# Probability products of an attention kernel issued for two tiles at a time instead of one

## The chip, the cores and the metric

The kernel runs on one core of a Trainium2 chip. The metric is the device time of one launch in microseconds (us). Three runs gave 1793.2, 1794.21 and 1794.51 us, median 1794.21. Below, PE is TensorE, DVE is VectorE, ACT is ScalarE, POOL is GpSimd, and SP issues the DMAs.

## The reference, cut to what matters

The input is 4 sequences (b) of 1024 tokens and width 512. A post-norm layer is computed: causal attention with 32 heads of 16 dimensions, then a linear layer on values rounded to 4 bits in blocks.

```python
q, k, v = x @ Wq.T, x @ Wk.T, x @ Wv.T         # 32 heads of 16; q, k get rotary positions
scores = einsum('bhid,bhjd->bhij', q, k) * scale
scores = scores + bias        # learnable, for 0 <= i - j < 256, and 0 outside that band
scores = where(i >= j, scores, -inf)
m = maximum(max(scores, -1), softmax_offset)
p = exp(scores - m)
denom = sum(p, -1) + exp(softmax_offset - m)
out = einsum('bhij,bhjd->bhid', p, v) / denom
x = layernorm(x + out @ Wo.T)
x = layernorm(x + quantised_linear(x))
```

The change is in how `p @ v` is ordered among the other products. Nothing else is touched.

## The kernel before, in words

There are three stages. Stage 1 (up to about 415 us) makes q, k and v and stores them. Stage 2 (about 415 to 1507 us) is the attention. Stage 3 is the two layer norms and the linear layer. The change is in stage 2 alone.

Stage 2 is 32 **steps**: 8 groups (g) of 4 heads, by 4 sequences (b), n = 4g + b. A step is cut into 12 **tiles** T. A tile is one block of 128 keys by up to 512 queries, transposed (keys on partitions), for all 4 heads. `TILES` gives the order: tiles 0 to 3 are the first 512 queries (512, 384, 256 and 128 queries wide, since the causal corner is left out), tiles 4 to 11 are the second 512 queries (512 wide for tiles 4 to 8, then 384, 256, 128). Ten of the twelve tiles touch the band in which the bias is not zero (`BANDED`, all but tiles 4 and 5).

A tile is worked off as two **units** u = 2T and 2T + 1, of two heads each, so a step has 24 units. The work of one step on each engine:

- PE, `scores` (lines 663 to 689): two score products (line 679), one per head, into the bank pair `ps_s[u % 2]`. There are two bank pairs, so scores of unit u wait until the exponential of unit u - 2 is done (line 669). For an even unit of a banded tile PE also adds the bias by two products with an identity (line 685). For an odd unit of a banded tile ACT has written the bias into the bank pair first (`seed`), and PE waits for that (line 676).
- ACT, `exp_unit` (lines 871 to 877): one exponential over both heads of the unit, from `ps_s` to `probs`, which holds three tiles. Behind an odd unit comes `seed` (lines 879 to 892) for the next tile: a fill with zeros outside the band (line 889) where the tile is wider than the band, and a copy of the bias (line 891). It needs the bank pair that the exponential just before it has emptied. Twice a step `copy_out` (line 903) empties the bank of the output.
- PE, `pv` (lines 691 to 703): the probability product of a tile, for 4 heads. Each head takes 32 of the 128 columns of the array (32 weights: 16 values and a row of ones), so the four heads' products run side by side. They are in fp32, which comes out as two passes, so a tile is 8 matmul records. They wait for the exponentials of both units of their tile, and accumulate into one bank `ps_o`.
- The **maxima** for the step after next: PE makes 48 score products per step into a ring of 3 banks (`maxima`, line 660), and DVE reduces each (`max_unit`, lines 1148 to 1170). PE may fill a bank only when DVE has read what stood in it three uses before (`wait_use`). `units_beside(u)` says which stand beside unit u: the first between the two heads' scores of the unit (`inner`), one or two more after the unit (`behind`). Units 22 and 23 have none, nor have the last two steps.
- The ring is used, too, by one transpose of the shifts per step (line 716, read by DVE in four dependent operations, lines 1195 to 1201) after unit 1, and by the transposes of the output (line 709, read by DVE's `normalise`, lines 1206 to 1219) after units 4 and 13.

The order on every engine is written out by hand: an engine does its instructions in this order and waits at each for semaphores. On PE, before the change, the probability product of tile T stands behind the scores of unit 2T + 3, that is at units 3, 5, ..., 23 for tiles 0 to 10; tile 11 stands at unit 1 of the next step (`PV_LEFT`). SP's loads for later steps wait for whole steps of scores and of probability products.

Of the kernel before, what the change touches and what calls it, by code (L numbers as in the profile page):

```python
# [58 lines left out]
NT = len(TILES)  # L59
# [4 lines left out]
def tile_cols(T):  # L64
    c, J = TILES[T]
    i0 = max(P * J, CH * c)
    return c, J, i0, CH * (c + 1) - i0


def band_cols(T):  # L70

    c, J, i0, w = tile_cols(T)
    b0 = i0 - P * J
    return b0, max(0, min(BAND - b0, w))
# [26 lines left out]
def units_beside(u):  # L101

    ks = list(range(min(NM, NM * u // SPREAD), min(NM, NM * (u + 1) // SPREAD)))
    return ks[:1], ks[1:]
# [61 lines left out]
def ahead(g, b, k=AHEAD):  # L166

    return (g, b + k) if b + k < B else (g + 1, b + k - B)
# [7 lines left out]
def slot_free(k, depth):  # L176

    return FIRST + k - depth + 1
# [34 lines left out]
def build(nc, hT, h, wqT, wkT, wvT, woT, bias, bias_rev, offset, wff, bff, cos, sin, out):  # L213
    ctx = ExitStack()
    with ctx:
# [209 lines left out]
        def before_in(g, b):  # L425
            return (g, b - 1) if b else (g - 1, B - 1)
# [181 lines left out]
        def _(pe):  # L608
# [37 lines left out]
            def wait_use(use):  # L646

                if not isinstance(use.before, int) or use.before >= RING:
                    pe.wait_ge(ring_read, use.before - RING + 1)

            def maxima(g, b, ks, use_of):

                for k in ks:
                    I, c0, c1 = MAX_UNITS[k % NMU]
                    hl = k // NMU
                    if k == 0:
                        pe.wait_ge(stack_loaded[b], 16 * 9 * (g + 1))
                    use = use_of(k)
                    wait_use(use)
                    pe.matmul(ps_ring[:, use.bank, 0:c1 - c0], q_stack[0:STACK, b, hl, I * P:(I + 1) * P],  # L660
                              k_stack[0:STACK, b, hl, c0:c1], start=True, stop=True).then_inc(ring_filled, 1)

            def scores(g, b, n, u, between):

                c, J, i0, w = tile_cols(u // 2)
                if u == 0:
                    pe.wait_ge(shift_loaded[b], 16 * PARTS * (g + 1))
                    pe.wait_ge(bias_split, 3 * (g + 1))
                pe.wait_ge(exp_done, slot_free(n * NU + u, 2))
                b0, bw = band_cols(u // 2)  # L670

                in_bank = bw and u % 2
                if in_bank:
                    pe.wait_ge(seeded, n * NBAND + BANDED.index(u // 2) + 1)
                for hh in range(2):
                    hl = 2 * (u % 2) + hh
                    mm = pe.matmul(ps_s[:, u % 2, hh, 0:w], k_stack[0:ROWS, b, hl, J * P:(J + 1) * P],  # L679
                                   q_stack[0:ROWS, b, hl, i0:i0 + w], start=not in_bank,  # L680
                                   stop=bool(in_bank or not bw), skip_group_check=bool(in_bank))
                    if bw and not in_bank:
                        for s in range(2):
                            rhs = bias_r[:, bass.ds(g % 2, 1), s, hl, b0:b0 + bw].rearrange("p a c -> p (a c)")
                            mm = pe.matmul(ps_s[:, u % 2, hh, 0:bw], ident_r[:, :], rhs,  # L685
                                           start=False, stop=(s == 1))
                    if hh == 0:
                        between()
                mm.then_inc(scored, 1)

            def pv(g, b, n, T):

                c, J, i0, w = tile_cols(T)
                pe.wait_ge(exp_done, FIRST + n * NU + 2 * T + 2)
                if T == 0:
                    pe.wait_ge(v_loaded[b % 2], 16 * (g * 2 + b // 2 + 1))
                if J == 0:
                    pe.wait_ge(o_copied, FIRST + n * 2 + c)
                for hl in range(HG):
                    mm = pe.matmul(ps_o[VW * hl:VW * (hl + 1), i0 - CH * c:CH],  # L700
                                   v_sb[:, b % 2, J, VW * hl:VW * (hl + 1)], probs[:, T % 3, hl, 0:w],
                                   start=(J == 0), stop=(T + 1 in T_OF_CHUNK))
                mm.then_inc(pv_done, 1)

            def transpose_out(n, c, use):
                pe.wait_ge(o_copied, FIRST + n * 2 + c + 1)
                wait_use(use)
                for i in range(4):
                    mm = pe.transpose(ps_ring[:, use.bank, i * P:(i + 1) * P],
                                      o_sb[:, c, i * P:(i + 1) * P], ident[:, :])  # L710
                mm.then_inc(ring_filled, 1)

            def transpose_shift(n, use):
                pe.wait_ge(shift_steps, 4 * n + 2)
                wait_use(use)
                pe.transpose(ps_ring[0:HG * NB, use.bank, 0:P], shift[:, :], ident[:, :]).then_inc(ring_filled, 1)
# [7 lines left out]
            def phase2(g, kind):  # L724
                last = kind == LAST_GROUP
                for b in range(B):
                    n = g * B + b
                    ga, ba = ahead(g, b)
                    more = not (last and b >= B - AHEAD)
                    left = b or kind != FIRST_GROUP  # L730

                    def use_of(what):
                        return Use(g, b, what, kind)

                    def use_before(what):
                        return Use(g, b - 1, what, kind)

                    for u in range(NU):
                        inner, behind = units_beside(u) if more else ((), ())
                        scores(g, b, n, u, lambda: maxima(ga, ba, inner, use_of))  # L740
                        if left and u == PV_LEFT:
                            pv(*before_in(g, b), n - 1, NT - 1)
                        if u % 2 and u > 1:
                            pv(g, b, n, u // 2 - 1)
                        maxima(ga, ba, behind, use_of)
                        if left and u == MT_LEFT and not (last and b > B - AHEAD):
                            transpose_shift(n + 1, use_before("M"))
                        if left and u == OT_LEFT:
                            transpose_out(n - 1, 1, use_before("O1"))
                        if u == OT_0:  # L750
                            transpose_out(n, 0, use_of("O0"))
                    if last and b == B - 1:
                        pv(g, b, n, NT - 1)
                        transpose_out(n, 1, use_of("O1"))

            groups(pe, phase2)


# [696 lines left out]
```

## Time and profile before

| | |
|---|---|
| time of the profiled execution | 1794.08 us |
| its span | 1792.3 us |
| median of the three runs | 1794.21 us |
| PE busy | 1639.8 us, 91% of the span, 9136 matmuls |
| DVE busy | 1291.7 us, 72% |
| ACT busy | 1109.9 us, 62% |
| probability products (line 700) | 3072 matmul records, mean 498 ns, four side by side |
| exponentials (line 876) | 768, 592.2 us busy |
| seeds (lines 889, 891) | 128 and 320, 70.0 and 197.1 us busy |
| maxima on DVE (lines 1159, 1166) | 364.6 and 501.6 us busy |

The profile is of one execution. Busy time is the union of an engine's instructions. Matmuls are pipelined: their records overlap, and what a matmul occupies is read from the distance of its start to the next start. The granted TensorE clock is at full speed (2.4 GHz) from 431.7 to 1523.9 us, that is for nearly all of stage 2, and at half of it for 75 us before that. One core has one queue of each engine, and no other core takes part.

### The profile page before, as it was taken

The numbers are of one execution on the slowest core, as the hardware profiler recorded it, in microseconds if no ns is written. First come the engines' busy times: TensorE is split into PE (matmuls) and PEld (weight loads), VectorE is DVE, ScalarE is ACT, GpSimd is POOL, SyncE is SP. The second block draws the span as 40 slices with busy tenths as digits, with TensorE's granted clock in tenths as the row PEclk, the third lists the DMA queues.
The fourth block names the chain that finished last, engine by engine and source line by source line (L and its number), as shares of the span: only waits on it lengthen the run. The fifth ranks groups of instructions, "written<-read, shape, count | busy, mean of one in ns | idle before, by whom it ended". The sixth has DMA issues, their size and how long they took to land. (4 is left out here: it accounts for less than half of the span.)

```text
span 1792.3 us, 28802 instructions
## 1 busy us (share of the span) xinstructions
PE 1639.8 (91%) x9136; PEld 762.4 (43%) x9136; DVE 1291.7 (72%) x3801; ACT 1109.9 (62%) x1596; POOL 249.4 (14%) x123
## 2 busy tenths in 40 slices
PE   7999999669999999999999999999999998777763
PEld 3444444213444444444444444444444443333321
DVE  2444544398887888888888788878888833589996
ACT  2333333205878778778887887877878886344432
POOL 4323323210000000000000000000000000244443
PEclk9999999858999999999999999999999999899995
DMA  5444444842453444335335334433533202122211
GB/s 210 141 156 155 140 160 151 193 95 48 84 85 60 84 72 73 80 64 84 80 58 90 81 53 78 93 58 66 105 57 57 53 15 76 35 77 76 70 47 47
DMA packets 124628, 157.09 MB, mean 88 GB/s; under 512 B 14928, under 2 KB 80528, under 8 KB 124240
## 3 DMA queue, kind: packets, MB, share of 16 engines
q1 hardware_dynamic: 124496, 155.45, 37.2%
q8 instruction: 68, 1.11, 0.3%
q14 instruction: 64, 0.52, 0.1%
HBM read 104.15 MB, written 50.46 MB: 86 GB/s over the span
## 5 line engine op out<-in xcount | busy, mean ns | idle before, releaser
L876 ACT ACTIVATE probs<-ps 128x1024 f32<-128x1024 f32 (+3 forms) x768 | 592.2, 810 | 176.7 <-PE ps L685 118.3
L1166 DVE CUSTOM_DVE_ANT_0 junk<-ps,bias_q 128x384 bf16<-128x384 f32 (+2 forms) x1024 | 501.6, 502 | 138.1 <-PE ps L660 127.6
L660 PE MATMUL ps<-k_stack,q_stack 96*128 96x384 bf16 (+3 forms) x1536 | 501.4, 344 | 30.8 <-DVE mx L1166 16.3
L679 PE MATMUL ps<-q_stack,k_stack 99*128 99x512 bf16 (+3 forms) x1536 | 489.6, 328 | 13.2 <-ACT ps L891 4.7
L1159 DVE TENSOR_REDUCE mx<-ps 128x1 f32<-128x128 f32 (+3 forms) x768 | 364.6, 485 | 42.4 <-PE ps L660 35.1
L685 PE MATMUL ps<-bias_r,ident_r 128*128 128x384 f32 (+2 forms) x1280 | 352.6, 363 | 0.0
L636 PE MATMUL ps<-attn 128*128 128x512 f32 x768 | 332.2, 595 | 10.9 <-DMA attn<-hT 9.9
L700 PE MATMUL ps<-probs,v_sb 128*32 128x512 f32 (+3 forms) x3072 | 327.3, 498 | 0.1
L660 PEld LDWEIGHTS ps<-k_stack,q_stack 96*128 96x128 bf16 x1536 | 143.0, 97 | 379.8 <-DVE mx L1166 149.8
L685 PEld LDWEIGHTS ps<-bias_r,ident_r 128*128 128x128 f32 x1280 | 222.4, 193 | 37.1 <-issue 0.3
L636 PEld LDWEIGHTS ps<-attn 128*128 128x128 f32 x768 | 146.5, 191 | 195.8 <-issue 195.8
L891 ACT ACTIVATE ps<-bias_s 128x768 f32<-128x768 f32 (+2 forms) x320 | 197.1, 616 | 23.0 <-ACT probs L876 0.8
L679 PEld LDWEIGHTS ps<-q_stack,k_stack 99*128 99x128 bf16 x1536 | 146.8, 98 | 97.1 <-issue 44.1
L790 PE MATMUL ps<-q_stack,k_stack 128*128 128x512 f32 x256 | 121.8, 631 | 22.6 <-ACT k_stack L947 16.7
L1034 POOL TENSOR_TENSOR probs<-attn 128x1024 f32<-128x1024 f32 x32 | 106.2, 3317 | 237.8 <-ACT attn L840 209.7
L1050 POOL CAST bias_r<-work 128x768 f32 (+1 forms) x8 | 6.6, 828 | 899.8 <-DMA work<-ext_k_dram 899.7
L1119 DVE TENSOR_TENSOR probs<-attn 128x1024 f32<-128x1024 f32 x32 | 39.2, 1225 | 104.1 <-ACT attn L840 92.1
L700 PEld LDWEIGHTS ps<-probs,v_sb 128*32 128x32 f32 x3072 | 60.5, 107 | 118.2 <-issue 96.6
L790 PEld LDWEIGHTS ps<-q_stack,k_stack 128*128 128x128 f32 x256 | 50.2, 201 | 84.9 <-issue 64.5
L1166 DVE DVE_READ_ACCUMULATOR2_ANT mx<- 128x1 f32 x1024 | 84.2, 82 | 0.0
L889 ACT ACTIVATE ps<-zero 128x256 f32<-128x256 f32 (+2 forms) x128 | 70.0, 547 | 14.8 <-ACT probs L876 0.4
L1125 DVE TENSOR_TENSOR probs<-probs 128x512 f32<-128x512 f32 x32 | 22.8, 712 | 74.6 <-POOL probs L1034 74.6
(90 smaller groups left out, 1068.6 us busy)
## 6 DMA issues: line engine op xcount, KB each, us to landing
q_stack<-q_parts SPq DMA_DIRECT2D x192, 128.0 KB, 4.3
v_dram<-v_sb SPq DMA_DIRECT2D x32, 512.0 KB, 2.7
v_sb<-v_dram SPq DMA_DIRECT2D x32, 512.0 KB, 9.6
q_parts<-q_stack SPq DMA_DIRECT2D x96, 128.0 KB, 1.9
k_parts<-k_stack SPq DMA_DIRECT2D x96, 128.0 KB, 2.0
k_stack<-k_parts SPq DMA_DIRECT2D x32, 384.0 KB, 7.3
attn<-hT SPq DMA_DIRECT2D x8, 1024.0 KB, 6.3
k_stack<-k_parts SPq DMA_DIRECT2D x32, 256.0 KB, 8.0
```

Of the source, the lines that this page charges most:

```text
L636: mm = pe.matmul(ps[:, bank, :], lhsT, rhs, start=(kt == 0), stop=(kt == NK - 1))
L660: pe.matmul(ps_ring[:, use.bank, 0:c1 - c0], q_stack[0:STACK, b, hl, I * P:(I + 1) * P], k_stack[0:STACK, b, hl, c0:c1], start=True, stop= ...
L679: mm = pe.matmul(ps_s[:, u % 2, hh, 0:w], k_stack[0:ROWS, b, hl, J * P:(J + 1) * P], q_stack[0:ROWS, b, hl, i0:i0 + w], start=not in_bank, ...
L685: mm = pe.matmul(ps_s[:, u % 2, hh, 0:bw], ident_r[:, :], rhs, start=False, stop=(s == 1))
L700: mm = pe.matmul(ps_o[VW * hl:VW * (hl + 1), i0 - CH * c:CH], v_sb[:, b % 2, J, VW * hl:VW * (hl + 1)], probs[:, T % 3, hl, 0:w], start=(J ...
L790: mm = pe.matmul(ps_y[:, w, :], at_T[par][:, w, kt * P:(kt + 1) * P], wo_sb[:, kt, :], start=(kt == 0), stop=(kt == NK - 1))
L876: act.activation(probs[:, (u // 2) % 3, 2 * pr:2 * pr + 2, 0:w], ps_s[:, pr, :, 0:w], ACT.Exp).then_inc(exp_done, 1)
L889: act.activation(ps_s[:, 1, :, bw:w], zero[:, :].unsqueeze(2).broadcast_to([P, 2, w - bw]), ACT.Copy)
L891: act.activation(ps_s[:, 1:2, :, 0:bw], bias_s[:, bass.ds(g % 2, 1), :, b0:b0 + bw], ACT.Copy)\
L1034: pool.tensor_tensor(by_sin[:, q % 2, :, :], raw[:, q % 2, :, :], rope_cs[:, 1, q % 2, c:c + 1, :].broadcast_to([P, 2, CH]), ALU.mult).the ...
L1159: ins = dve.tensor_reduce(mx[:, par, hl, I, slot:slot + 1], ps_ring[:, use.bank, 0:far], AX.X, ALU.max)
L1166: ins = dve.tensor_tensor_reduce(out=junk[:, use.bank, 0:c1 - lo], in0=ps_ring[:, use.bank, lo - c0:c1 - c0], in1=bias_q[:, hl, BAND - t0 ...
```

## The change

On PE, the probability products of two tiles are issued together. Tiles 0 and 1 stand behind the scores of unit 5, tiles 2 and 3 at unit 9, 4 and 5 at unit 13, 6 and 7 at unit 17, 8 and 9 at unit 21, and tiles 10 and 11 at unit 1 of the next step. So units 3, 7, 11, 15, 19 and 23 have none. The instructions are the same and as many. All other engines' programs are unchanged. In the last step tiles 10 and 11 come after unit 23.

```diff
@@ -738,10 +738,13 @@
                     for u in range(NU):
                         inner, behind = units_beside(u) if more else ((), ())
                         scores(g, b, n, u, lambda: maxima(ga, ba, inner, use_of))
+
                         if left and u == PV_LEFT:
-                            pv(*before_in(g, b), n - 1, NT - 1)
-                        if u % 2 and u > 1:
-                            pv(g, b, n, u // 2 - 1)
+                            for T in (NT - 2, NT - 1):
+                                pv(*before_in(g, b), n - 1, T)
+                        if u % 4 == 1 and u > 1:
+                            for T in (u // 2 - 2, u // 2 - 1):
+                                pv(g, b, n, T)
                         maxima(ga, ba, behind, use_of)
                         if left and u == MT_LEFT and not (last and b > B - AHEAD):
                             transpose_shift(n + 1, use_before("M"))
@@ -750,7 +753,8 @@
                         if u == OT_0:
                             transpose_out(n, 0, use_of("O0"))
                     if last and b == B - 1:
-                        pv(g, b, n, NT - 1)
+                        for T in (NT - 2, NT - 1):
+                            pv(g, b, n, T)
                         transpose_out(n, 1, use_of("O1"))
```

## Rows read from the trace of the kernel before

**Rows 1.** Busy time of one step: start:end, length, then each engine.

```profile
863.50:897.85 34.35, 34.02 (x246) 16.38 (x243) 28.10 (x102) 27.45 (x42) 3.41 (x3) 1.00 0.49 104
```

**Rows 2.** Waits in that step: who waited for whom, us in total, times, longest.

```profile
PEld ps L660 <- DVE mx L1159: 4.0, 7, 0.8
```

**Rows 3.** Timeline of PE around one probability product: start us, length us, instruction.

```profile
902.43 0.33 PE L660 MATMUL ps<-k_stack,q_stack 96*128 96x384 bf16 x1
902.59 0.33 PE L679 MATMUL ps<-q_stack,k_stack 99*128 99x384 bf16 x1
902.85 1.06 PE L700 MATMUL ps<-probs,v_sb 128*32 128x512 f32 x8
...
903.30 0.61 PE L700 MATMUL ps<-probs,v_sb 128*32 128x512 f32 x4
903.85 0.34 PE L660 MATMUL ps<-k_stack,q_stack 96*128 96x384 bf16 x1
```

**Rows 4.** Timeline of PE, first scores of unit 13 in two successive steps.

```profile
881.59 0.38 PE L679 MATMUL ps<-q_stack,k_stack 99*128 99x512 bf16 x1
...
915.94 0.38 PE L679 MATMUL ps<-q_stack,k_stack 99*128 99x512 bf16 x1
```

**Rows 5.** Timeline of PE and ACT, second scores of unit 14 to unit 17.

```profile
884.47 0.38 PE L679 MATMUL ps<-q_stack,k_stack 99*128 99x512 bf16 x1
...
888.68 0.38 PE L679 MATMUL ps<-q_stack,k_stack 99*128 99x512 bf16 x1
...
885.12 1.94 ACT L876 ACTIVATE probs<-ps 128x1024 f32<-128x1024 f32 x2 [0.53 <-PE ps L685]
...
887.50 0.80 ACT L891 ACTIVATE ps<-bias_s 128x768 f32<-128x768 f32 x1
```

**Rows 6.** Timeline of PE and ACT, second scores of unit 18 to unit 21.

```profile
891.25 0.33 PE L679 MATMUL ps<-q_stack,k_stack 99*128 99x384 bf16 x1
...
894.75 0.27 PE L679 MATMUL ps<-q_stack,k_stack 99*128 99x256 bf16 x1
...
891.96 1.51 ACT L876 ACTIVATE probs<-ps 128x768 f32<-128x768 f32 x2 [0.50 <-PE ps L685]
893.59 0.60 ACT L891 ACTIVATE ps<-bias_s 128x512 f32<-128x512 f32 x1
```

**Rows 7.** Timeline of ACT and PE: last seed of a step, first scores of unit 1.

```profile
898.32 0.80 ACT L891 ACTIVATE ps<-bias_s 128x768 f32<-128x768 f32 x1
...
899.27 0.38 PE L679 MATMUL ps<-q_stack,k_stack 99*128 99x512 bf16 x1
```

**Rows 8.** Timeline of ACT: the seed before unit 13.

```profile
915.42 0.37 ACT L891 ACTIVATE ps<-bias_s 128x256 f32<-128x256 f32 x1
```

**Rows 9.** Timeline of PE and DVE, units 1 to 5.

```profile
900.31 0.39 PE L660 MATMUL ps<-k_stack,q_stack 96*128 96x512 bf16 x1
...
901.30 0.33 PE L679 MATMUL ps<-q_stack,k_stack 99*128 99x384 bf16 x1
...
905.57 0.27 PE L679 MATMUL ps<-q_stack,k_stack 99*128 99x256 bf16 x1
...
900.74 0.29 DVE L1159 TENSOR_REDUCE mx<-ps 128x1 f32<-128x128 f32 x1 [0.18 <-PE ps L660]
...
902.50 0.40 DVE L1159 TENSOR_REDUCE mx<-ps 128x1 f32<-128x256 f32 x1
```

**Rows 10.** Timeline of PE and DVE, units 5 to 9.

```profile
906.89 0.45 PE L660 MATMUL ps<-k_stack,q_stack 96*128 96x512 bf16 x2
...
907.65 0.22 PE L679 MATMUL ps<-q_stack,k_stack 99*128 99x128 bf16 x1
...
910.27 0.38 PE L679 MATMUL ps<-q_stack,k_stack 99*128 99x512 bf16 x1
...
907.39 0.28 DVE L1159 TENSOR_REDUCE mx<-ps 128x1 f32<-128x128 f32 x1
...
909.42 0.55 DVE L1166 CUSTOM_DVE_ANT_0 junk<-ps,bias_q 128x384 bf16<-128x384 f32 x1
```

## The prediction

> **What bounds the kernel now.** I read the page's totals first, then the busy times of one step, then the waits, and last the timelines of PE, ACT and DVE side by side. In one step of 34.35 us PE has 34.02 us busy, DVE 28.10, ACT 27.45 [rows 1]: PE looks like the bound, and the change shortens PE's own work. But records of matmuls overlap, so a busy PE may still be waiting. The reader is to see two things. First, PE's weight loads for the maxima wait 4.0 us per step for DVE, though PE has other work in flight during most of it [rows 2]: the ring of three banks is often full. Second, at some places of the step PE stands at the far end of a chain through ACT. The bias copy before unit 1 ends at 899.12 and unit 1 starts at 899.27 [rows 7]; the one before unit 13 ends at 915.79 and unit 13 starts at 915.94 [rows 4, 8]. Both times the gap is 0.15 us, so ACT sets these starts already, with a probability product inside the stretch. So PE bounds the step on average, with two cushions: two bank pairs of scores towards ACT, three ring banks towards DVE. The question is whether these carry a PE that works unevenly.
>
> **What the change removes.** Starts of neighbours give the price of going into and out of the products of 32 columns. From a 384-column product of the maxima to the next score product it is 902.59 - 902.43 = 0.16 us; from an equally wide score product to the probability product 902.85 - 902.59 = 0.26: 0.10 to go in. From pass to pass it is 903.30 - 902.85 = 0.45, from the second pass to the next other product 903.85 - 903.30 = 0.55: 0.10 to go out [rows 3]. Each is a difference of rounded starts; I take 0.09 for each, so a group that goes saves 0.18. Six go per step: 1.1 us, 35.5 us over 32 steps. This holds if the second tile follows at the pitch of a pass. No row shows two tiles back to back without a wait; the bound below is nothing saved, the bound above all 0.18. I take all: within a tile the second pass comes without a gap, and its wait for the exponentials is the one that unit's scores have passed.
>
> **What it moves.** A product of a 512-wide tile takes 2 x 0.45 = 0.90 to 0.91 us without its way in and out. A 256-wide one has passes of half the streaming, (0.45 - 0.03) / 2 + 0.03 = 0.24, so 0.48 (0.03 is what 0.45 has over 1024 columns at 2.4 GHz). Removed as a group of its own, a 512-wide tile gives PE 0.91 + 0.18 = 1.09. The moved ones are tiles 0, 4, 6, 8 (512 wide) and 2, 10 (256 wide), each from two units earlier to the place of its follower. Tile 3 still is at unit 9, tile 11 at unit 1, so the copies of the output start no later than ACT gets to them. A buffer of probabilities comes free at unit 2T - 1 for an odd-numbered use, before the scores of unit 2T: no new wait on ACT. SP's queue waits for steps as a whole, and the last product of a step stays where it was: about 0.5 us later, and the load of v that waits for it has the rest of the step to land. That delay I cost at nothing.
>
> **The step in six stretches.** Let a stretch go from the scores of unit u = 1, 5, 9, 13, 17, 21 (where the pair stands) to those of unit u + 4. Part A runs to the second score product of unit u + 1 and contains the pair; part B is the rest, in which no probability product is left. During the pair ACT can finish only what is in its two bank pairs and DVE what is in its three ring banks; then both run dry. So B can't shrink below the chain that starts afresh in unit u + 1.
>
> Part A grows by the moved product whole: 0.91 at u = 5, 13, 17, 21 and 0.48 at u = 1, 9, in sum +4.60 us.
>
> Part B shrinks by less than what PE is relieved of:
> - u = 13: before, 888.68 - 884.47 = 4.21 us. The ACT chain in it: the exponential of unit 14 starts 885.12 - 884.47 = 0.65 after the scores; two exponentials, zero fill and bias copy run without a pause to 887.50 + 0.80 = 888.30; 0.15 later unit 17 may start. That is 3.98 [rows 5, 7]. PE would be relieved of 1.09 and can use 0.23.
> - u = 17: before, 894.75 - 891.25 = 3.50. Chain: 0.71 + (893.59 + 0.60 - 891.96 = 2.23) + 0.15 = 3.09 [rows 6]. Gain 0.41 of 1.09.
> - u = 21: the chain (exponentials 22 and 23, zero fill, bias copy) ends B already [rows 7]. Gain 0.
> - u = 9: as well [rows 4, 8]. The copy of the output stands ahead of the exponential of unit 10 and will have gone by then; the ring takes most of that back. Gain 0.1.
> - u = 1: DVE. The third maximum's fill (900.31) reaches DVE at 900.74, then come its two reductions and the four operations on the shifts, and the reduction of the next bank ends at 902.50 + 0.40 = 902.90, 2.59 after the fill [rows 9]. Some 0.06 later (the gap where a fill waits for a reduction in the same timeline) PE may fill the second bank of unit 3, so 2.65. In the trace of before the product of tile 0 hides this; it goes. From that fill to unit 5 it is 905.57 - 903.85 = 1.72 [rows 3, 9], and 0.15 more where the output's transposes wait for their bank behind a late DVE: 1.87. The fill comes 901.30 - 900.31 = 0.99 before part B, so B is 2.65 + 1.87 - 0.99 = 3.53, before 905.57 - 901.30 = 4.27. Gain 0.74.
> - u = 5: DVE. From the first fill after the pair to the end of the reductions that unit 8's second bank needs it is 0.43 (as from 900.31 to 900.74) + (909.42 + 0.55 - 907.39 = 2.58) = 3.01, then 0.06 and 0.17 to unit 9: 3.24. The fill comes 907.65 - 906.89 = 0.76 before B, 0.07 of it a wait for a bank that goes: 0.69. So B is 2.55, before 910.27 - 907.65 = 2.62 [rows 9, 10]. The product of tile 2, which leaves here, was hiding DVE and no more. Gain 0.07.
>
> In sum B shrinks by 0.23 + 0.41 + 0 + 0.10 + 0.74 + 0.07 = 1.55. The step grows by 4.60 - 1.55 = 3.05 us, from 915.94 - 881.59 = 34.35 [rows 4] to 37.4. Put otherwise: PE saves 1.1 and waits about 4.1 more.
>
> Steps 1 to 29 are alike. Steps 30 and 31 have no maxima; ACT's chains are then the bound all the more, and I take the same 3.05. Step 0 has no pair at unit 1 and begins at half clock, where PE is slower than the others: half. So 31 x 3.05 + 1.5 = 96 us. Stages 1 and 3 don't change. The profiled execution took 1794.1 us (0.1 below the median of the runs), so I forecast 1890 us, 5.3% slower.
>
> The Trainium skill, TensorEngine Tiling (Array Packing), PSUM Bottleneck, says that packing speeds up TensorE but not the emptying of PSUM. By it, too, PE's gain isn't the step's. The trace agrees: the engines that empty the banks set the starts of units 1 and 13 [rows 7, 8].
>
> **The rivals.**
> 1. PE is the bound and the cushions suffice: 35.5 us less, 1758.6 us. For it: 34.02 of 34.35 busy [rows 1]. Against it: units 1 and 13 start on ACT's word today [rows 4, 7, 8], so taking PE work out of those stretches can give nothing, while the pair adds to the part before. It decides if the moved product can be worked off while ACT still has 0.9 us of work queued; two bank pairs allow that only where ACT is behind, and ACT has idled 0.53 us before unit 14 [rows 5]. The Trainium skill, TensorEngine Tiling (Array Packing), Key Properties, says that changing the tiling mode drains TensorE; by that rule half as many changes make the time shorter, by the same six per step. The two 0.1 us steps at the product's edges agree with it [rows 3].
> 2. Only ACT's chains bind and DVE keeps up. For it: 28.10 of 34.35 busy [rows 1]. Then B at u = 1 and u = 5 would shrink by PE's relief as far as ACT allows, about 0.6 and 0.9 us per step more: 30 x 1.5 = 45 less, 1845 us. Against it are the waits of rows 2.
> 3. The second tile doesn't follow without a gap, the change does half of what it says: 6 x 0.09 x 32 = 17 us more, 1907; with 0.18 each 1925 us. No row speaks for a gap.
> 4. PE's savings and the new waits cancel: 1794 us, within 0.2% (3.6 us, about what a measurement of this kernel tells from no change). It needs chains three quarters shorter than their rows.
>
> **How the numbers follow.** Forecast 0.70, rival 1 0.06, rival 2 0.13, rival 3 0.08, rival 4 0.03. The forecast's own spread is 0.5 us per step either way, since a wait can begin or end between my stretches: 1874 to 1906. The range takes in most of rivals 2 and 3: 1848 to 1912. Faster by over 0.2%: 0.06; within: 0.03; slower: 0.91.
>
> **What would show it.** Right: unit 13 to unit 13 takes about 37.4 us; from the start of a pair of 512-wide tiles to the next other product 1.90 us; unit 17 starts 0.15 us after the end of its bias copy and 3.98 after unit 14's second scores; unit 1 likewise, with the stretch from unit 21 to unit 1 longer by 0.9; waits of PE's weight loads for DVE grow; ACT idles over 1.3 us before unit 14's exponential. The clock stays at 2.4 GHz, since no wait of PE in stage 2 is expected over 1 us. Wrong: a step below 34.35 us, with unit 17 starting well after its bias copy (rival 1); unit 9 not waiting for DVE (rival 2); over 1.95 us for such a pair (rival 3).

## The result, and the profile after

The changed kernel takes 1888.95 us (median of 4 runs, 1888.18 to 1889.37), the kernel before 1794.36. The ratio is 1.0528, 95% interval 1.051 to 1.0546. The forecast was 1890. In the profiled executions the span grew from 1792.3 to 1887.2 us. Of these 94.9 us, 0.9 lie before the first step and nearly all the others in stage 2.

The page of the changed kernel: busy time by engine, then the exponentials with ACT's idle time before them.

```profile
PE 1649.6 (87%) x9128; PEld 772.6 (41%) x9136; DVE 1290.3 (68%) x3801; ACT 1114.2 (59%) x1596; POOL 249.3 (13%) x123
...
L880 ACT ACTIVATE probs<-ps 128x1024 f32<-128x1024 f32 (+3 forms) x768 | 599.0, 807 | 266.7 <-PE ps L685 197.1
```

Work is the same on all engines; lines of ACT and DVE have moved by 4. ACT's idle time before its exponentials grew from 176.7 to 266.7 us. One step of the changed kernel, from unit 13 to unit 13 (start:end, length, then PE, weight loads, DVE, ACT, POOL, granted clock, DMA), and its longest waits for DVE:

```profile
882.35:919.47 37.12, 34.31 (x241) 16.66 (x242) 28.05 (x102) 27.58 (x42) 0.00 (x0) 1.00 0.32 58
```

```profile
PEld ps L660 <- DVE mx L1163: 2.9, 7, 0.7
PEld ps L660 <- DVE mx L1170: 2.1, 6, 0.6
```

In the kernel before, the line of [rows 2] had this one beside it:

```profile
PEld ps L660 <- DVE mx L1166: 3.7, 7, 0.8
```

So these waits of the weight loads were 4.0 + 3.7 us a step before and are 2.9 + 2.1 now. They didn't grow; they don't measure what PE loses, as the run with a fast DVE shows below.

Against [rows 1] the step is 2.77 us longer with nearly the same busy time of DVE and ACT: the three engines overlap less. PE's busy 34.31 hides this, since records overlap.

The stretches behind the pairs, PE and ACT, to be held against [rows 5] and [rows 6]:

```profile
882.35 0.38 PE L679 MATMUL ps<-q_stack,k_stack 99*128 99x512 bf16 x1 [0.65 <-ACT ps L895]
...
882.98 1.92 PE L700 MATMUL ps<-probs,v_sb 128*32 128x512 f32 x16
884.84 0.34 PE L660 MATMUL ps<-k_stack,q_stack 96*128 96x384 bf16 x1
...
886.09 0.38 PE L679 MATMUL ps<-q_stack,k_stack 99*128 99x512 bf16 x1
...
890.06 0.38 PE L679 MATMUL ps<-q_stack,k_stack 99*128 99x512 bf16 x1 [0.41 <-ACT ps L895]
...
893.48 0.33 PE L679 MATMUL ps<-q_stack,k_stack 99*128 99x384 bf16 x1
...
896.56 0.27 PE L679 MATMUL ps<-q_stack,k_stack 99*128 99x256 bf16 x1 [0.22 <-ACT ps L895]
```

```profile
886.74 1.94 ACT L880 ACTIVATE probs<-ps 128x1024 f32<-128x1024 f32 x2 [1.39 <-PE ps L685]
888.80 0.39 ACT L893 ACTIVATE ps<-zero 128x256 f32<-128x256 f32 x1
889.12 0.80 ACT L895 ACTIVATE ps<-bias_s 128x768 f32<-128x768 f32 x1
...
894.18 1.51 ACT L880 ACTIVATE probs<-ps 128x768 f32<-128x768 f32 x2 [1.43 <-PE ps L685]
895.81 0.60 ACT L895 ACTIVATE ps<-bias_s 128x512 f32<-128x512 f32 x1
```

The pair (16 records) runs from 882.98 to the next other product at 884.84. ACT, idle for 1.39 us (0.53 before) until the scores of unit 14 are there, starts its chain afresh at 886.74 and ends it at 889.12 + 0.80 = 889.92; unit 17 starts 0.14 later. Between 886.09 and 890.06 PE has 3.1 us of its own (the length of this stretch in the run below with both neighbours fast) and waits for the rest. The same again to unit 21, which starts 0.15 us after its bias copy ends (895.81 + 0.60 = 896.41).

The stretch that DVE ends, to be held against [rows 9]: PE's waits in unit 3, and DVE's rows that end them.

```profile
905.42 0.33 PE L679 MATMUL ps<-q_stack,k_stack 99*128 99x384 bf16 x1
906.06 0.34 PE L660 MATMUL ps<-k_stack,q_stack 96*128 96x384 bf16 x1 [0.31 <-DVE mx L1163]
```

```profile
903.84 0.29 DVE L1163 TENSOR_REDUCE mx<-ps 128x1 f32<-128x128 f32 x1 [0.61 <-PE ps L660]
...
905.60 0.40 DVE L1163 TENSOR_REDUCE mx<-ps 128x1 f32<-128x256 f32 x1
```

DVE reads the unit's second bank until 905.60 + 0.40 = 906.00; 0.06 later PE fills it. Medians over steps 5 to 27, in us, part A with the pair and part B behind it as the prediction cut them:

| stretch from unit | A before | A after | B before | B forecast | B after |
|---|---|---|---|---|---|
| 1 | 2.03 | 2.46 | 4.27 | 3.53 | 3.63 |
| 5 | 2.09 | 2.87 | 2.61 | 2.55 | 2.55 |
| 9 | 1.66 | 2.10 | 4.01 | 3.91 | 3.92 |
| 13 | 2.88 | 3.74 | 4.21 | 3.98 | 3.97 |
| 17 | 2.56 | 3.42 | 3.50 | 3.09 | 3.08 |
| 21 | 2.00 | 2.85 | 2.52 | 2.52 | 2.52 |

Part A grew by 4.22, part B shrank by 1.45: 2.77 us a step. Over the run, from the starts of the steps: 0.9 us before the first, 2.5 in step 0, 80.9 in steps 1 to 29 (two of them grew by 0.26 and 0.28 more than the others), 6.0 in step 30, 4.9 in step 31, and 0.2 less behind it: 95.0 by these rounded terms. The 0.9 is no work of the change: in the kernels of this study whose stage 1 is as before, the first step starts at 415.8 to 417.1 us.

### The profile page after: what moved, and what is told of

Its sections match the earlier page's. It is cut to its first block and busy times, and to the rows that moved or that the text cites. A ratio compares the mean times of both kernels' runs of the same rounds, so it can differ in the third digit from the quotient of the medians.

```text
span 1887.2 us, 28794 instructions
## 1 busy us (share of the span) xinstructions
PE 1649.6 (87%) x9128; PEld 772.6 (41%) x9136; DVE 1290.3 (68%) x3801; ACT 1114.2 (59%) x1596; POOL 249.3 (13%) x123
## 3 DMA queue, kind: packets, MB, share of 16 engines
q1 hardware_dynamic: 124496, 155.45, 35.5%
## 5 line engine op out<-in xcount | busy, mean ns | idle before, releaser
L880 ACT ACTIVATE probs<-ps 128x1024 f32<-128x1024 f32 (+3 forms) x768 | 599.0, 807 | 266.7 <-PE ps L685 197.1
L700 PE MATMUL ps<-probs,v_sb 128*32 128x512 f32 (+3 forms) x3072 | 291.0, 496 | 0.0
L700 PEld LDWEIGHTS ps<-probs,v_sb 128*32 128x32 f32 x3072 | 80.4, 109 | 152.8 <-issue 113.1
```

The source lines that it names most:

```text
L880: act.activation(probs[:, (u // 2) % 3, 2 * pr:2 * pr + 2, 0:w], ps_s[:, pr, :, 0:w], ACT.Exp).then_inc(exp_done, 1)
```

## Experiments

Each expectation was on record before its run. Theory: PE works ahead of ACT by two bank pairs and of DVE by three ring banks. A pair keeps PE away for longer than these last, and the relief in the units without a product is lost to chains through ACT and DVE. Rivals: ACT's chain or DVE's ring alone; pairs are slow in themselves; only their place is at fault. No run gave PE more banks, so that their number sets the loss is argued from the chains, not shown. The kernel before took 1793.6 to 1794.0 us on the chips of these runs; ratios are to it. Changed and control kernel of a couple ran on one chip.

**ACT's bias copies away.**

```diff
-                in_bank = bw and u % 2
-                if in_bank:
-                    pe.wait_ge(seeded, n * NBAND + BANDED.index(u // 2) + 1)
+                bw = 0 if u % 2 else bw
+                in_bank = False
...
-            seed(0, 0)
...
-                        seed_after(g, n, u, (g,) if b < B - 1 else () if last else (g + 1,))
```

> The kernel before without ACT's zero fills and bias copies for the odd units (the bias of the odd units' heads is left out of the result; the matmuls are as many). It is the control for the next run. My theory (the step ends on chains exponential, bias copy, scores two units on): the waits of PE for bias copies in a step of before, 0.10 before unit 1, 0.28 before unit 3 and 0.29 before unit 13, go: 0.67 x 32 = 21 us less, 1773 us (1765 to 1785). Rival, DVE's ring alone binds: 1790 or more.

> The changed kernel, with the same taken out. Theory: in a step of it PE waits 0.17 before unit 1, 0.83 before unit 13, 0.57 before unit 17 and 0.40 before unit 21 for bias copies; the stretch before unit 17 keeps a part because scores wait for a bank pair. 1.7 us a step less, 1834 us (1820 to 1850), so 61 us above its control in place of 94. Rival A, DVE alone is the cause: 94 us above the control as before. Rival B, ACT's bias copies alone are: at or below the control.

Measured: control 1769.2 us (ratio to before 0.9861, 0.9845 to 0.9878), changed 1817.6 (1.0132, 1.0115 to 1.0148): 48.4 us apart in place of 94.6, so both rivals fall. A step takes 33.72 against 35.20 us. By stretch, changed less control: +0.07, +0.72, -0.19, +0.04, +0.05, +0.78. The stretches from units 9, 13 and 17, which had lost 0.35, 0.62 and 0.43, lose 0.05 at most. That from unit 21 goes on losing: there the scores of unit 0 wait 0.43 us for unit 22's exponential. The bias copies carry 2.77 - 1.48 = 1.3 us of the loss. The changed kernel came out 16 us below what I expected: its steps are 1.92 us shorter where I had said 1.7, and the rest is in steps 0, 30 and 31, which I had reckoned like the others and which got 3.0, 7.0 and 6.0 us shorter.

**DVE fast.**

```diff
-                    ins = dve.tensor_reduce(mx[:, par, hl, I, slot:slot + 1], ps_ring[:, use.bank, 0:far],
+                    ins = dve.tensor_reduce(mx[:, par, hl, I, slot:slot + 1], ps_ring[:, use.bank, 0:min(far, 64)],
...
+                    few = min(c1 - lo, 64)
...
-                        out=junk[:, use.bank, 0:c1 - lo], in0=ps_ring[:, use.bank, lo - c0:c1 - c0],
-                        in1=bias_q[:, hl, BAND - t0 - 1::-1], scale=1.0, scalar=LOWEST, op0=ALU.add, op1=ALU.max,
+                        out=junk[:, use.bank, 0:few], in0=ps_ring[:, use.bank, lo - c0:lo - c0 + few],
+                        in1=bias_q[:, hl, BAND - t0 - 1::-1][:, 0:few], scale=1.0, scalar=LOWEST, op0=ALU.add, op1=ALU.max,
```

> The kernel before with DVE's reductions of the maxima over at most 64 columns of each block (the maxima leave the others out; as many instructions). Control for the next run. Theory: PE's waits for a ring bank in a step (0.08 and 0.27 in unit 6, 0.12 in unit 10) go: 0.4 to 0.5 a step, 1780 us (1774 to 1790).

> The changed kernel with the same fast DVE. Theory: the stretch from unit 1 to 5 falls back to ACT's chain (0.5 less) and the one from 5 to 9 to PE's own work (0.85 less), the four others stay, since ACT ends them: 1.45 a step less than the changed kernel, 1846 us (1832 to 1860), 66 us above its control. Rival A, DVE alone is the cause: at or below the control. Rival B, ACT alone: still 94 above it.

Measured: control 1769.4 us (0.9864, 0.9847 to 0.988), changed 1828.9 (1.0196, 1.0179 to 1.0213): 59.5 apart. Both are lower than expected by the same cause: the maxima of steps 0 and 1, made ahead of the first step, are DVE's, and the first step began at 401.3 in place of 416.8 us (control: 401.7 for 415.9). A step is 34.02 against 35.61: DVE carries 2.77 - 1.59 = 1.2 us. In the control a step is only 0.33 us shorter than before, for all that weight loads waited 4.0 + 3.7 us a step for DVE there. Part B from unit 1 is 3.15 and from unit 5 1.70; the other four stayed within 0.01 but the one from unit 9 (3.75 for 3.92). What is left above PE's own work in the stretch from unit 1 is a wait before unit 4, PE and ACT:

```profile
870.89 0.33 PE L660 MATMUL ps<-k_stack,q_stack 96*128 96x384 bf16 x1
871.30 0.28 PE L679 MATMUL ps<-q_stack,k_stack 99*128 99x256 bf16 x1
```

```profile
870.44 0.80 ACT L880 ACTIVATE probs<-ps 128x768 f32<-128x768 f32 x1
```

The scores of unit 4 come 0.41 us after a product that elsewhere is followed after 0.16 [rows 3]: they need the bank pair of unit 2, whose exponential ends at 870.44 + 0.80 = 871.24. These 0.25 us are just what this part B (3.15) is above the one with both neighbours fast (2.90). So where DVE lets go ACT's chain is next, by an exponential and not by the bias copy.

**PE almost alone.** The two edits above, and the exponentials over 64 columns at most:

```diff
-                act.activation(probs[:, (u // 2) % 3, 2 * pr:2 * pr + 2, 0:w], ps_s[:, pr, :, 0:w],
+                few = min(w, 64)
+                act.activation(probs[:, (u // 2) % 3, 2 * pr:2 * pr + 2, 0:few], ps_s[:, pr, :, 0:few],
```

> The kernel before with both engines beside PE made fast: no fills and bias copies for odd units, reductions and exponentials over at most 64 columns (most of the probabilities are then stale, and the bias of half the heads is left out). PE's instructions are the same. Control for the next run. Theory: PE alone is left, its waits of 1.66 us a step go: about 1742 us (1735 to 1755).

> The changed kernel with the same. Theory: the saving that the change makes on PE alone comes out whole: 6 ways in and out at 0.18 a step, and the pitch of passes in a pair, 1.1 to 1.35 us a step, 35 to 43 us below its control, about 1702 us. Rival, a pair is itself slow on PE or the saving isn't there: level with the control or above.

Measured: control 1736.5 us (0.9683, 0.9667 to 0.9699), changed 1707.25 (0.9517, 0.9502 to 0.9533). The control's time is within what was expected, but not for my reason: its step is 33.21 us, 1.14 shorter and not 1.66, and its first step begins 14.7 us earlier because DVE's maxima are fast. With fast neighbours the change makes the kernel 29 us faster: the saving exists, and pairs aren't slow. It is 6 us short of the least that was expected. A step is 32.26 for 33.21; a wait is left in it, before unit 0, for the exponential of unit 22. It takes 0.48 by difference: the stretch from unit 21 is 0.18 shorter than the control's, where that from unit 5, relieved of a 256-wide tile too, is 0.67 shorter. With that the saving on PE is 0.95 + 0.48 = 1.4 a step, 0.23 to 0.24 per group: 0.18 for the way in and out, and 0.05 because passes that follow others of 32 columns have a pitch of 0.43, not 0.45.

**The two tiles apart, at the same unit.**

```diff
+                            two = [(before_in(g, b), n - 1, T) for T in (NT - 2, NT - 1)]
                         if u % 4 == 1 and u > 1:
-                            for T in (u // 2 - 2, u // 2 - 1):
-                                pv(g, b, n, T)
-                        maxima(ga, ba, behind, use_of)
+                            two = [((g, b), n, T) for T in (u // 2 - 2, u // 2 - 1)]
+                        for at, m, T in two[:1]:
+                            pv(*at, m, T)
+                        maxima(ga, ba, behind[:1], use_of)
+                        for at, m, T in two[1:]:
+                            pv(*at, m, T)
+                        maxima(ga, ba, behind[1:], use_of)
```

> The changed kernel with the first maximum behind the unit put between the two tiles' products, so that both tiles stand at the same unit but are not adjacent. Theory: each pair loses its saving, 0.18 to 0.23 x 6 = 1.1 to 1.4 a step, and DVE gets a bank 0.4 to 0.9 us earlier, which gives back up to 0.9 a step in the two stretches that DVE ends: 1904 us (1885 to 1925). Rival, DVE starved during the pair is the main cost: 20 us or more below the changed kernel's 1889.

Measured: 1908.5 us (1.0646, 1.0628 to 1.0664), 19.6 over the changed kernel. Part A is 0.24 longer in each of the six stretches (0.28 in one), part B 0.46 shorter from unit 1 and 0.26 from unit 5; these are near what was expected (1.5 lost and 0.8 given back in all six stretches). The saving of a merged pair is real in the full kernel, too; it lies in part A, and bunching costs more.

**The pairs one unit earlier.**

```diff
+                            for T in {0: (10, 11)}.get(u, ()):
                                 pv(*before_in(g, b), n - 1, T)
...
+                        for T in {4: (0, 1), 8: (2, 3), 12: (4, 5), 16: (6, 7), 20: (8, 9)}.get(u, ()):
+                            pv(g, b, n, T)
```

> The pairs one unit earlier, behind the scores of units 4, 8, 12, 16, 20 and of unit 0 of the next step, where PE also waits for the exponential before. Theory: from odd unit to odd unit there is ACT's chain (exponential, fill, bias copy: 2.5 to 2.9 us where tiles are wide), and a pair here too leaves every second such interval with 1.8 us of PE work; but ACT has a bias copy and an exponential queued when the pair begins. In a wide stretch I reckon 7.4 us, between 7.09 of before and 7.71 of after: 1835 us (1810 to 1860). Rival A, only the late place is at fault: 1794 or less. Rival B, any pair costs alike: 1889.

Measured: 1902.1 us (1.0607, 1.0589 to 1.0625). I was wrong by 67 us, and rival A falls. Rival B gave 1889 and the measured time is 13 us above it, so the place matters here too. DVE and PE around the pair at unit 12:

```profile
925.36 0.08 DVE L1169 DVE_READ_ACCUMULATOR2_ANT mx<- 128x1 f32 x1
927.29 0.29 DVE L1162 TENSOR_REDUCE mx<-ps 128x1 f32<-128x128 f32 x1 [1.85 <-PE ps L660]
```

```profile
925.01 1.92 PE L700 MATMUL ps<-probs,v_sb 128*32 128x512 f32 x16
926.87 0.39 PE L660 MATMUL ps<-k_stack,q_stack 96*128 96x512 bf16 x1
...
927.31 0.27 PE L660 MATMUL ps<-k_stack,q_stack 96*128 96x256 bf16 x1
...
927.64 0.33 PE L660 MATMUL ps<-k_stack,q_stack 96*128 96x384 bf16 x1
928.20 0.63 PE L709 MATMUL ps<-ident,o_sb 128*128 128x128 f32 x4 [0.23 <-DVE mx L1169]
```

DVE had one bank left when the pair began and idled 1.85 us. Behind the pair come three fills within 0.8 us (926.87 to 927.64), because the odd unit has no bias products between them, and PE waits for DVE. I had reckoned with ACT alone. DVE isn't all of the miss, though: the six stretches are 1.02, 0.54, 0.78, 0.52, 0.27 and 0.18 us longer than before, and in the first of them, the longest, PE waits 0.36 us for a bias copy before unit 3 and 0.26 for an exponential before unit 4.

**One pair only.**

In both, a table of the units at which the tiles' products stand takes the place of the rule of before. The line that differs, first for tiles 4 and 5, then for 0 and 1:

```diff
+                        for T in {3: (0,), 5: (1,), 7: (2,), 9: (3,), 13: (4, 5), 15: (6,), 17: (7,), 19: (8,), 21: (9,), 23: (10,)}.get(u, ()):
```

```diff
+                        for T in {5: (0, 1), 7: (2,), 9: (3,), 11: (4,), 13: (5,), 15: (6,), 17: (7,), 19: (8,), 21: (9,), 23: (10,)}.get(u, ()):
```

> The kernel before with one pair only: tile 4's product leaves unit 11 and joins tile 5's at unit 13. Theory: ACT's chain ends the stretch that it leaves (unit 13 starts 0.15 after the bias copy), so nothing is gained there, and unit 14 comes later by the product, 0.86: 31.5 x 0.86 = 27 us, 1821 us (1815 to 1826). Rival, the cost is one of pairs as such, a sixth of 94.6 us each: 1810.

> The kernel before with one pair only: tile 0's product leaves unit 3 and joins tile 1's at unit 5. Theory: unit 5 comes 0.64 earlier (as in the changed kernel, until DVE ends that stretch), then 0.78 is added, 0.14 a step: 4.5 us, 1799 us (1794 to 1805). Rival, a sixth of the loss: 1810.

Measured: tiles 4 and 5 together 1826.5 us (1.0185, 1.0171 to 1.0199), 0 and 1 together 1800.6 (1.0041, 1.0028 to 1.0055). The costs of pairs differ by a factor of almost five, as their places say. In the first, a step is 0.86 longer, all in the stretch from unit 13. PE and ACT before it, where tile 4's product is gone:

```profile
892.12 0.39 PE L660 MATMUL ps<-k_stack,q_stack 96*128 96x512 bf16 x1
893.26 0.38 PE L679 MATMUL ps<-q_stack,k_stack 99*128 99x512 bf16 x1 [0.74 <-ACT ps L892]
```

```profile
891.99 0.81 ACT L890 ACTIVATE ps<-zero 128x768 f32<-128x768 f32 x1
892.74 0.37 ACT L892 ACTIVATE ps<-bias_s 128x256 f32<-128x256 f32 x1
```

893.26 is 0.15 after 892.74 + 0.37, as before the change [rows 4, 8]: a product of 1.09 us was taken away and unit 13 starts no sooner after the bias copy. Steps 1 to 29 give 25 us; 1826.5 is above my 1821 mainly by the last two steps, 2.5 and 2.9 us longer in the profiled executions where I had reckoned 0.86 each; the granted clock was at half for 3.4 us of the one and 6.8 us of the other, of which more below. In the second a step is 0.16 longer (expected 0.14).

**The maxima first.** In the changed kernel, and in the one before, the line of the maxima behind the unit goes ahead of the probability products.

```diff
+                        maxima(ga, ba, behind, use_of)
                         if left and u == PV_LEFT:
...
-                        maxima(ga, ba, behind, use_of)
```

> The changed kernel with the pair behind the maxima that follow the unit, so that DVE has two or three banks to read while the pair runs. Theory: DVE's share of the loss goes: 0.5 a step in the stretch from unit 1 to 5, 0.3 in the one from 5 to 9 (0.85 less 0.55 in which the second fill waits for the output's transpose to be read), nothing in the four that ACT ends: 25 us below the changed kernel, 1864 us (1850 to 1880). Rival, DVE's idle time in the pair is made up anyway: 1889.

> The kernel before with the same order: single products behind the maxima that follow the unit. DVE idles 0.5 us in unit 4 and 1.1 in unit 13 of a step because a product holds back the fill of its bank. Theory: only its waits in units 3 to 10 (0.5 a step) can shrink, by a part, since DVE is without a pause there: 0 to 0.3 a step, 1788 us (1780 to 1796). Rival, no part of it: 1794.

Measured: 1887.9 us (1.0519, 1.0501 to 1.0536) and 1835.1 (1.0231, 1.0217 to 1.0245). Both missed: with pairs 24 us of the 25 expected didn't come, and with single products the kernel is 41 us slower. With pairs the stretch from unit 1 is 0.47 shorter, as expected, but the one from unit 5 is 0.45 longer: there the second fill waits 0.44 us until the output in its bank is read, and the pair stands behind it. With single products a step is 35.71 us, 1.36 longer; 0.44 of it is in the stretch from unit 5, 0.43 in that from unit 17 and 0.41 in that from unit 21. PE at unit 5 of the latter, and DVE:

```profile
889.37 0.39 PE L660 MATMUL ps<-k_stack,q_stack 96*128 96x512 bf16 x1
890.21 0.23 PE L660 MATMUL ps<-k_stack,q_stack 96*128 96x128 bf16 x1 [0.45 <-DVE attn L1217]
890.37 0.85 PE L700 MATMUL ps<-probs,v_sb 128*32 128x384 f32 x8
```

```profile
889.72 0.42 DVE L1217 TENSOR_TENSOR attn<-ps,rden 128x256 f32<-128x256 f32 x1
```

The second fill waits until 889.72 + 0.42 = 890.14 for its bank, and the product, which was ready, stands in the queue behind it. At units 17 and 21 the last fill waits for one of DVE's reductions in the same way (0.26 and 0.21 us), with the product behind it. In these places the product was what PE did while DVE caught up. No version that does all the work beats the kernel before.

## Why the prediction was right

- *ACT and DVE set the starts behind a pair.* Right, and to 0.01 us in five of six parts B. The chains read off the trace of before held unchanged: taking ACT's copies away, or DVE's time, moved the stretches named. Each alone carries less than half of 2.77 us; with both gone and the exponentials short, the change gains 29 us.
- *Nothing is gained where ACT ends the stretch.* Right; the run with tiles 4 and 5 alone shows it by itself. The Trainium skill, TensorEngine Tiling (Array Packing), PSUM Bottleneck, says that tiling speeds up TensorE but not the emptying of PSUM. The trace agrees: part B from unit 21, which ACT ended before, is 2.52 us with and without the product of tile 10 in it.
- *The rivals.* The first (1758.6 us) needed cushions that carry PE, but behind four of the six pairs PE waits for ACT and behind the two others for DVE. The third needed over 1.95 us for a pair, which takes 1.86. The second, DVE keeps up, is wrong: with pairs, fills in units 3 and 8 wait for DVE. Its price was well read, for with a fast DVE the parts B from units 1 and 5 are 0.48 and 0.85 shorter where it said 0.6 and 0.9.
- *The price of going in and out, 0.18.* Right, and 0.05 too small per pair: the pitch of the passes is the term that was mis-sized. I had priced a moved 512-wide tile at 0.91 and a 256-wide one at 0.48; they measure 0.86 and 0.43 (0.78 at unit 5, where a wait went too). So part A grew by 4.22, not 4.60. The pair runs 884.84 - 882.98 = 1.86 us, not 1.90. The 35.5 us for six groups in 32 steps are a slip besides: 6 x 0.18 x 32 is 34.6.
- *Part B from unit 1.* 3.63 for 3.53. I counted 0.15 for the wait of the output's transposes; in the step there are waits of 0.22 and 0.03 there.
- *The weight loads' waits for DVE grow.* They fell, from 7.7 to 5.0 us a step, while DVE's part in the loss was as forecast. This sign was wrong: such a wait counts time in which PE still has work in flight.
- *The step.* 37.12 for 37.40, so 29 steps gave 80.9 us in place of 88.5.
- *Step 0.* 2.5 us for 1.5. The times of the granted clock in the section on the profile before count from another zero than the timelines. On the timelines' scale the clock is at full speed from 420.5 to 1512.8 us, so that only the first 4.6 us of step 0 are at half clock, and there was little reason to halve its loss.
- *Steps 30 and 31 as the others.* Wrong: 6.0 and 4.9 us, not 3.05 each. It is luck that this and step 0 cancelled what the 29 steps gave too little: the total is 1 us off, its largest term 7.6. I had said that no wait of PE in stage 2 is over 1 us and that the clock stays up. The first was not so even before the change, where step 30 has this wait, with the clock at full speed all through the step:

```profile
1463.34 0.59 PE L679 MATMUL ps<-q_stack,k_stack 99*128 99x512 bf16 x2 [1.10 <-ACT ps L891]
```

In the changed kernel neither held. Step 30, where no maxima fill PE's gaps:

```profile
1546.10 0.39 PE L679 MATMUL ps<-q_stack,k_stack 99*128 99x512 bf16 x1 [0.80 <-ACT probs L880]
...
1548.34 1.01 PE L679 MATMUL ps<-q_stack,k_stack 99*128 99x512 bf16 x2 [1.27 <-ACT ps L895]
1549.28 3.64 PE L700 MATMUL ps<-probs,v_sb 128*32 128x512 f32 x16
```

```profile
1547.40:1554.20 6.80, 5.86 (x24) 1.93 (x25) 0.18 (x1) 3.88 (x6) 0.00 (x0) 0.50 0.00 0
```

The granted clock is 0.50, that is 1.2 GHz, from 1547.40, behind the wait of 0.80 and within the one of 1.27 us, and the pair takes 3.64 us for 1.92. The Trainium skill, TensorE: Matmul & The Clock Gate, What's actually happening, says that the throttled clock is the default and activity releases it. The trace agrees as far as it goes: the clock is at half for 75 us up to 421 us, at full through the busy steps, and at half again here.

What this costs can be read in part. The run with the pairs behind the maxima has in steps 30 and 31, which have no maxima, the same instructions on PE, and the same waits of 0.80 and 1.27 us in step 30, but there its clock was at half for 3.4 us only:

```profile
1549.80:1553.20 3.40, 3.40 (x19) 0.99 (x12) 0.00 (x0) 1.92 (x3) 0.00 (x0) 0.50 0.00 0
```

Its step 30 takes 34.75 us for 35.88, all of the difference in the stretch from unit 13: 8.96 for 10.09 (before: 6.45). So 3.4 us more of half clock cost 1.1 us. The other parts of step 30 grew by 2.3 us together. In the couple without bias copies the clock stayed at full in both last steps, and they grew by 2.3 us each. A price comes from the run with the pairs one unit earlier, too, in one step far from the end:

```profile
1333.60:1337.00 3.40, 3.40 (x22) 1.18 (x21) 1.82 (x6) 1.02 (x1) 0.00 (x0) 0.50 1.06 143
```

This step takes 39.21 us where its neighbours, the same but at full clock, take 37.66: 3.4 us of half clock cost 1.55 us. How much of the remaining 8.96 - 6.45 us is the clock and how much the longer wait isn't shown: no kernel with tiles 4 and 5 together at unit 13 and with its bias copies kept the clock up in the last two steps.

## What to carry to other kernels

Before work of the bound engine is bunched, read how much work its neighbours have queued when the bunch begins, and what is the shortest chain through them behind it: a stretch is the bunch plus the longer of that chain and the engine's own work, and relief below the chain is worth nothing. Here PE was relieved of 5.7 us a step behind the pairs (by the couple with fast neighbours) and could use 1.45. An engine with 99% of busy time may still be waiting: before the change a step was 1.14 us longer than with fast neighbours. Such waits show in the distance from start to start; look for starts at a constant distance after another engine's end, and check that the distance goes when that engine's work goes. And a ready piece of work must not stand in a queue behind one that waits: the single products of the kernel before cost little just where they fall in time in which PE would wait.

## What the runs showed of the hardware that was not expected

- The fp32 products of 32 columns of two tiles follow each other without a gap, and from the second pass on the pitch over 512 columns is 0.43 us, where the first pass after other products takes 0.45 (passes of the pair start at 882.98, 883.44, 883.87 and 884.29): a pair of 512-wide tiles takes 1.86 us to the next other product, two single ones 2 x 1.00 and 0.09 for the second way in.
- Where PE waits for them, it restarts 0.06 us after DVE's reduction ends (905.60 + 0.40 to 906.06) and 0.14 to 0.15 after ACT's bias copy (889.12 + 0.80 to 890.06), in all kernels of this study that have such waits.
- In the last two steps the clock fell to half behind or within waits of PE of 0.80 and 1.27 us (step 30 above). The waits of 0.71 and 1.10 us in step 30 of the kernel before, and of 0.65 us before unit 13 of the changed one (the row of 882.35), left it at full speed. The length of one wait doesn't settle it: with the pairs one unit earlier the clock fell once, at 1333.6 us, among waits of at most 0.45 us, and in no other of the like steps.
